# Attention scores in two 64-row halves, and scores, values and turns at the head of each slot

## The reference

```python
x = x + fast_weights(layernorm(x))      # 16 steps in order: z, y = x@t_k.T, x@t_v.T; one gradient step
                                        # on W1, b1, W2, b2 from mean((z + gelu(z@W1.T+b1)@W2.T+b2 - y)**2);
                                        # then the updated network on x@t_q.T
x = x + block(layernorm(x))

def block(x):                           # 16 heads, 4 key/value heads, 64 features a head
    q, k, v = split(rmsnorm(x) @ qkv_w + qkv_b)
    q, k = rope(q), rope(k)
    logits = q @ k.T / sqrt(64)         # a key at most 128 tokens back, none ahead
    attn = exp(logits - logaddexp(logsumexp(logits), attn_sink))
    x = x + (attn @ v) @ proj_w + proj_b
    h2 = rmsnorm(x)                     # then 4 of 32 experts for each token
    gw, e = softmax(top4(h2 @ gate_w + gate_b))
    return x + sum(gw * (silu(g) * u) @ W_down[e])    # u, g = halves of h2 @ W_up[e]
```

## Time and profile before

| | |
|---|---|
| time of the kernel, median of 3 runs | 1179.05 us (1175.15 to 1180.01) |
| profiled execution: span from first to last instruction | 1177.7 us (no other time of this execution is recorded) |
| PE busy, PEld busy | 981.5 us (83%), 716.8 us (61%) |
| DVE busy | 844.2 us (72%) |
| ACT busy | 629.5 us (53%) |
| POOL busy | 484.6 us (41%) |
| mean granted TensorE clock | 0.929 of full speed |

### The profile page before, as it was taken

How to read it: one execution, slowest core, us unless ns; L and a number is a source line. 1 busy time by engine, 2 the same in 40 slices (tenths; PEclk the granted TensorE clock), 3 DMA queues, 4 the chain that set the end, 5 groups by cost and what they waited for, 6 DMA issues and landing times. The chain is left out here.

```text
span 1177.7 us, 21481 instructions
## 1 busy us (share of the span) xinstructions
PE 981.5 (83%) x6262; PEld 716.8 (61%) x6356; DVE 844.2 (72%) x3032; ACT 629.5 (53%) x2211; POOL 484.6 (41%) x644
## 2 busy tenths in 40 slices
PE   4789999999999999899999989998895598797700
PEld 2446767666666666676666767666463487686600
DVE  3548898989888898989889898987883344333307
ACT  1027665665757576665757666575662155444300
POOL 2221214342433424243342534334234277777760
PEclk7799999999999999999999999999997699889955
DMA  5910000000000000000000000000083244443129
GB/s 143 265 29 1 2 1 21 1 21 1 21 11 11 19 3 21 1 21 8 14 15 7 21 1 20 7 15 19 3 300 131 71 129 131 133 113 99 54 67 334
DMA packets 65541, 67.29 MB, mean 57 GB/s; under 512 B 14961, under 2 KB 50706, under 8 KB 65426
## 3 DMA queue, kind: packets, MB, share of 16 engines
q1 hardware_dynamic: 51858, 44.13, 12.6%
q0 software_dynamic: 9216, 19.68, 4.9%
q10 hardware_dynamic: 4352, 2.10, 0.6%
HBM read 30.34 MB, written 35.52 MB: 56 GB/s over the span
## 5 line engine op out<-in xcount | busy, mean ns | idle before, releaser
L1137 POOL TENSOR_TENSOR l_t_cos<-l_t_cos,l_t_sin 128x512 f32<-128x512 f32 (+1 forms) x96 | 104.1, 1085 | 390.7 <-DVE l_t_sin L830 390.7
L1002 ACT ACTIVATE l_prob<-l_score,l_nm 128x256 f32<-128x256 f32 (+1 forms) x512 | 213.1, 439 | 1.8 <-DVE l_nm L697 1.5
L1331 POOL DMA_INDIRECT expert_out<-e_yo,e_dest x160 | 153.2, 957 | 68.8 <-issue 37.2
L1013 ACT COPY l_probT<-l_turned 128x512 f32<-128x512 f32 x192 | 112.9, 588 | 126.3 <-PE l_turned L388 125.7
L690 DVE TENSOR_REDUCE l_mx<-l_score 128x2 f32<-128x512 f32 (+1 forms) x192 | 131.6, 685 | 53.3 <-PE l_score L372 46.4
L96 POOL DMA_INDIRECT expert_rows<-h,slot x128 | 126.6, 989 | 47.7 <-issue 34.6
L388 PE MATMUL l_turned<-ident_sb,l_prob 128*128 128x128 f32 x768 | 122.8, 283 | 25.1 <-DVE l_prob L679 25.1
L679 DVE TENSOR_SCALAR l_prob<-l_prob,l_rec 128x256 f32<-128x256 f32 (+1 forms) x512 | 136.8, 321 | 6.8
L372 PE MATMUL l_score<-l_kpad,l_qT 128*128 128x512 f32 x256 | 131.5, 595 | 3.0
L404 PE MATMUL l_turned<-l_probT,l_vv 128*64 128x128 f32 x1536 | 126.5, 286 | 2.3 <-ACT l_probT L1013 2.3
L404 PEld LDWEIGHTS l_turned<-l_probT,l_vv 128*64 128x64 f32 x1536 | 80.0, 136 | 66.8 <-ACT l_probT L1013 39.7
(11 more groups left out here) (243 smaller groups left out, 1969.4 us busy)
## 6 DMA issues: line engine op xcount, KB each, us to landing
expert_rows<-zeros SPq DMA_DIRECT2D x32, 350.0 KB
e_xt<-expert_rows SPq DMA_DIRECT2D x160, 70.0 KB
e_rows<-expert_out SPq DMA_DIRECT2D x16, 512.0 KB, 5.9
wup_sb<-in_wup SPq DMA_DIRECT2D x1, 4096.0 KB, 14.7
expert_out<-e_yo,e_dest POOLq DMA_INDIRECT x160
expert_rows<-zeros SPq DMA_DIRECT2D x32, 70.0 KB, 2.4
expert_rows<-h,slot POOLq DMA_INDIRECT x128, 2.3
out_x<-e_res ACTq DMA_DIRECT2D x16, 128.0 KB, 6.1
```

What stands on the lines that cost most here:

```text
L1002: ins = A_.activation(prob[:, b, cols], score[u % 3][:, cols], ACT.Exp, bias=nm[:, b, j:j + 1], scale=0.125, accum_out=sums[:, b, j:j + 1])
L1013: A_.copy(probT[:, u % 2, :], turned[u % 2][:]).then_inc(s["probT"], 1)
L1137: g.tensor_tensor(t_cos[:, c % 2, 0:w], t_cos[:, c % 2, 0:w], t_sin[:, c % 2, 0:w], ALU.add).then_inc(s["added"], 1)
L1331: g_.indirect_dma_start(m["ys"], bass.IndirectOffsetOnAxis(ap=dest[:, g % FOUND, j:j + 1], axis=0), yo[:, g % YO, j, :], None).then_inc(se ...
```

## The change

Scores become two matmuls of 64 rows. `mask(u)` starts the tile; `half_scores(u, 0)` multiplies partitions 0 to 63 of the queries with head A's keys into the left half of the tile, `half_scores(u, 1)` partitions 64 to 127 with head B's into the right half. Neither reads the zeros of `kpad`. In slot u the program issues the mask and head A's half of unit u + 3, and beside it head B's half of unit u + 2, which goes to another bank. Head B's half signals that a tile is done. In tiles of the first queries the four blocks now stand head by head, so `nm`, `es` and the block numbers in `values` follow.

On PE the order inside a slot becomes scores, values, turns, and then `qkv`, the side stages and `qk_turn`. On ACT it becomes `exps(u + 1)`, `take_y(u - 1)`, `take_probs(u)`. DVE's order stays.

```diff
--- before.py
+++ after.py
@@ -292,7 +292,7 @@
             "stat small norms hn hn_ps hT qkv_ps cos sin added qk_ps qk_out v_out "
-            "s_ps mx nm es_in exped den rec normed t_ps probT y_ps yT "
+            "half_ps s_ps mx nm es_in exped den rec normed t_ps probT y_ps yT "
             "proj_ps xx x2 ss rms2 h2 h2_ps h2T gate_ps glog top w_in wexp wrec idx idxf hot picked rank_ps "
             "place prod masksum slotf slot x_sum counted").split()
@@ -355,28 +355,39 @@
             def bias(dst, c0, c1):
                 mm(dst, m["ones_bf"][:], m["bias3"][:, c0:c1], start=True, stop=False)
-            def scores(n, par, u):
+            def mask(n, par, u):
                 A, ap, u, done = at_unit(n, par, u)
                 if not live(A):
                     return
-                pairs, second, _ = unit(u)
-                g2 = pairs[0] // 4
-                dst = score[u % 3]
                 if u == 0:
                     pe.wait_ge(s["qk_out"], A * CHUNKS + 4)
                 if u == 6 or (u == 2 and A == 0):
                     pe.wait_ge(s["qk_out"], A * CHUNKS + CHUNKS)
                 after(pe, s["exped"], done - 3)
+                mm(score[u % 3][:], m["ident_bf"][:], (m["mask2"] if unit(u)[1] else m["mask1"])[:],
+                   start=True, stop=False)
+            def half_scores(n, par, u, hh):
+                A, ap, u, done = at_unit(n, par, u)
+                if not live(A):
+                    return
+                pairs, second, _ = unit(u)
+                g2, rows = pairs[0] // 4, slice(hh * DH, (hh + 1) * DH)
+                dst = score[u % 3][:, hh * 2 * P:(hh + 1) * 2 * P]
+                if hh == 1:
+                    pe.wait_ge(s["half_ps"], done)
                 if second:
-                    mm(dst[:], m["ident_bf"][:], m["mask2"][:], start=True, stop=False)
-                    mm(dst[:], qT[:, ap, pairs[0], P:TOK], kpad[:, ap, g2, :, :], start=False, stop=True) \
-                        .then_inc(s["s_ps"], 1)
+                    ins = mm(dst, qT[rows, ap, pairs[0], P:TOK], kpad[rows, ap, g2, hh, :], start=False, stop=(hh == 1))
                 else:
-                    mm(dst[:], m["ident_bf"][:], m["mask1"][:], start=True, stop=False)
                     for k, p in enumerate(pairs):
-                        ins = mm(dst[:, k * 2 * P:(k + 1) * 2 * P], qT[:, ap, p, 0:P], kpad[:, ap, g2, :, 0:P],
-                                 start=False, stop=(k == 1))
-                    ins.then_inc(s["s_ps"], 1)
+                        ins = mm(dst[:, k * P:(k + 1) * P], qT[rows, ap, p, 0:P], kpad[rows, ap, g2, hh, 0:P],
+                                 start=False, stop=(hh == 1 and k == 1))
+                ins.then_inc(s["s_ps"] if hh else s["half_ps"], 1)
+            def scores(n, par, u):
+                mask(n, par, u + 3)
+                half_scores(n, par, u + 3, 0)
+                half_scores(n, par, u + 2, 1)
             def turn_probs(n, par, u):
                 A, ap, u, done = at_unit(n, par, u)
@@ -398,7 +409,7 @@
                 for k in range(2):
                     for hh in range(2):
                         g = 2 * g2 + hh
-                        blk = 2 * hh + k if second else 2 * k + hh
+                        blk = 2 * hh + k
                         dst = turned[u % 2][hh * DH:(hh + 1) * DH, 0:P] if second else \
                             turned[u % 2][hh * DH:(hh + 1) * DH, k * P:(k + 1) * P]
                         ins = mm(dst, vv[:, ap, k if second else 0, g * DH:(g + 1) * DH],
@@ -632,22 +643,23 @@
             def iteration(n, par):
                 for u in range(UNITS):
-                    scores(n, par, u + 2)
+                    last_first = n == 2 and u == UNITS - 1
+                    if not last_first:
+                        scores(n, par, u)
+                    values(n, par, u - 1)
+                    turn_probs(n, par, u)
                     if n == 2 and u == 0:
                         qkv(n, par, 0)
                     if n == 2 and u % 2 == 0 and u < UNITS - 2:
                         qkv(n, par, u // 2 + 1)
                     elif n != 2 and u % 2 == 0:
                         qkv(n, par, u // 2)
-                    if u > 5 and u % 2 == 1:
-                        values(n, par, u - 1)
                     for stage in side.get(u, []):
                         stage(n, par)
-                    if not (u > 5 and u % 2 == 1):
-                        values(n, par, u - 1)
                     if u % 2 == 1:
                         qk_turn(n, par, u // 2)
-                    turn_probs(n, par, u)
+                    if last_first:
+                        scores(n, par, u)
                     if n < 3 or n == SEQS + 3:
                         keep_clock(1, turned[0] if n < 3 else score[2])
@@ -685,7 +697,10 @@
                 if live(A):
                     cols = unit(u)[2]
                     b, w = u % 2, cols.stop - cols.start
-                    sink = m["negsink"][:, cols]
+                    sink = m["negsink"][:, cols].rearrange("p (k h) -> p h k", h=2)
+                    def heads(tile):
+                        return tile[:, b, 0:w].rearrange("p (h k) -> p h k", h=2)
                     v.wait_ge(s["s_ps"], done)
                     V.tensor_reduce(mx[:, b, 0:w], score[u % 3][:].rearrange("p (h k) -> p h k", h=w), AX.X,
                                     ALU.max).then_inc(s["mx"], 1)
@@ -694,10 +709,10 @@
                 if live(A):
                     v.wait_ge(s["mx"], done)
-                    V.scalar_tensor_tensor(out=nm[:, b, 0:w], in0=mx[:, b, 0:w], scalar=-0.125, in1=sink,
+                    V.scalar_tensor_tensor(out=heads(nm), in0=heads(mx), scalar=-0.125, in1=sink,
                                            op0=ALU.mult, op1=ALU.min).then_inc(s["nm"], 1)
                     v.wait_ge(s["nm"], done)
-                    V.tensor_tensor(es[:, b, 0:w], nm[:, b, 0:w], sink, ALU.subtract).then_inc(s["es_in"], 1)
+                    V.tensor_tensor(heads(es), heads(nm), sink, ALU.subtract).then_inc(s["es_in"], 1)
             def x_norm(n, par):
@@ -1112,9 +1127,9 @@
             def iteration(n, par):
                 for u in range(UNITS):
-                    take_probs(n, par, u - 1)
-                    take_y(n, par, u - 2)
                     exps(n, par, u + 1)
+                    take_y(n, par, u - 1)
+                    take_probs(n, par, u)
                     if u in (0, 2):
                         v_out(n, par, u // 2)
                     if u % 2 == 1:
```

## The result

The changed kernel takes 1352.07 us (median of 4 runs, 1347.82 to 1353.77) against 1178.43 us of the kernel before beside it: a ratio of 1.1471, 95% interval 1.1451 to 1.149. The profiled span is 1350.6 us, 172.9 longer than before.

The account below looks back on a forecast made before the run. DVE was taken to bound the kernel: 47.25 us active plus 11.5 of waits gave 58.75, clock falls of 3.2 made 61.95, 10.0 more an iteration. 120 + 20 - 2 = 138 on 1179 gave 1317 us, range 1245 to 1360.

Parts of the forecast that it names:

- The rope loop: Even slots: DVE's rope waits for `qkv`, now behind the turns; 1.98 less 0.60 covered, 1.38 each, 8.3 an iteration.
- PE late in slots 2 and 4: PE reaches the turns late, 1.8 in slot 2 and 0.3 in slot 4, together 2.1 us an iteration.
- The gate's 0.7: Slot 7: `pick` waits for the gate, which now stands behind the turns; 0.7 us an iteration.
- The old waits: DVE's earlier waits for POOL and ACT, kept at 0.4 an iteration; those for scores were to go.
- DVE's active time: DVE's iteration time outside waits, 51.95 - 4.7 = 47.25 us, taken to stay the same.
- the prediction's own signs of being wrong: DVE's waits under 4.7 an iteration, `qkv` starting before `normed`, or DVE's active time leaving 47 us.
- The clock, 3.2: Falls after PE's pauses: 1.4 in slot 6, 0.6 each at slots 7, 9, 11; one fall at most 1.7.
- Three shorter iterations: Iterations 3, 16 and 17, with the same six rope waits but fewer side stages: 20 us at two thirds.
- the first rival: Rope waits without the clock's falls: 12 x 6.8 + 14 - 2 = 94 more, 1273 us; chance 0.22.
- The halves: PE's two 64-row score matmuls run side by side, 1.50 a unit for 1.79: 0.29 saved, mostly where PE waits anyway.
- The rival that the lighter PE wins: Slots 1 to 4, where DVE waits for PE: 3.5 us an iteration saved, 1134 us; chance 0.06.
- ACT's order at nothing: ACT's new order only makes its copies earlier, with ACT busy 33.45 of 51.95: priced at nothing.

Follow-up runs that it names:

- the filled kernel: The changed kernel with 10, 5, 8 and 7 extra matmuls ahead of PE's wait for the turns of slots 5, 7, 9 and 11: 1272.9 us, ratio 1.0811.
- the last kernel above: The kernel before, full-width scores, with DVE's rope ahead of the maxima in slots 0, 6, 8 and 10: 1167.95 us, ratio 0.9919.

## Why the prediction was right

It named the right mechanism and the right side, and 1352 lies in its range above the forecast of 1317. By its steps:

- **The rope loop, 1.38 an even slot: right.** Where PE is in time (slots 0, 6, 8 and 10 at full clock) the wait is 1.29; the 1.98 from the maxima to the rope were 1.97, and of these the maxima cover 0.68, not the 0.60 that the prediction took off. The six are 8.0 for the predicted 8.3, PE's lateness in slots 2 and 4 included. Moving `qkv` alone gives most of the time back.
- **PE late in slots 2 and 4, 2.1: right in place, a little high.** Slot 2 has 1.4 as a wait of the maxima for scores and a rope wait of 1.51, 0.2 above 1.29; slot 4 has 1.38, 0.1 above. Together 1.8. So the sentence that waits on scores would be gone was wrong: 8.0 us of two iterations are such waits, the rest of them behind falls of the clock. The gate's 0.7 is 0.63.
- **The old waits, 0.4: too high** (none is left in the list). All waits at full clock are 10.1, not 11.5.
- **DVE's active time, 47.25: too low** by 0.6 at full clock (57.97 less 10.1) and by 0.9 in the changed kernel (63.15 less 15.0 is 48.1). This is one of the prediction's own signs of being wrong, and it came. Its cause stays open. `es` is longer in the mean (598 ns, before 513; 16 us over 192 of them), as it now meets all six additions of POOL in an iteration. But before, the sixth fell on L795, the scaling of `l_hn`, which is shorter now (L810: 335 ns, before 773; 14 us over 32), so the two nearly cancel.
- **The clock, 3.2: the term that was mis-sized; it is 5.2.** The step that failed took 1.7 for the most that a fall can cost. Against the filled kernel, slot by slot, DVE's waits in the two iterations grow by 2.4 (slot 0), 1.5 and 2.5 (slot 6), 1.3 (7), 1.0 (8) and 1.0 (10). The longer falls at slots 5 and 11 cost more than 1.7: 3.8, in slots 6 and 7 of the longer iteration together, and 2.4 in slot 0. At slots 7 and 9 the price of 0.6 held in the mean: 1.0 each, in every other iteration.
- **Three shorter iterations, 20: measured 33.8** (12.2, 13.1, 8.5). Against the filled kernel the falls hold 17.9 of it; the 15.9 left are near the 14 that the first rival had for them. Iteration 18 gave 0.3 in place of -2, and 4.3 lie at the attention's start and in the experts, which the sum did not have. With 14.5 from the twelve full iterations, 13.8, 2.3 and 4.3 make the 34.9 by which the forecast was short. In the full iterations part of the closeness is luck: waits 1.4 too high stand against a clock 2.0 and an active time 0.6 too low.
- **The halves: right.** Side by side, 1.53 a unit for 1.50. Their 0.29 helps where PE has no reserve, three places an iteration by the prediction: 0.87, measured 0.73 at full clock. The rival that the lighter PE wins failed worse than its chance said, since under the new order, at the granted clock, the lighter PE loses.
- **ACT's order at nothing:** in the changed kernel no matmul of the two iterations waits for ACT, so the price holds there, but not for the reason given. It holds because PE's order changed with it.

The rival without falls of the clock, 1273, is what the filled kernel measured (1272.9); this is luck, as its twelve full iterations were together 9 us too dear and the rest as much too cheap.

The Trainium skill (TensorE: Matmul & The Clock Gate, Part 3), which the prediction named for a rival, says that matmuls on distinct row groups run at the same time. The trace after agrees with its starts of 427.27 and 427.28.

## What to carry to other kernels

Before a stage is moved behind an instruction that waits, look for who waits for that stage: if it is the engine that releases the wait, a loop closes, and its price is the sum of the stages in it less what still covers them. When two engines wait for each other in turn, price PE's pauses too, as the lower clock behind them cost here two thirds of what the rope loop did, and work saved on PE can make them longer. Orders of two engines that hand work to each other are one edit: ACT's half alone cost 31 us here, and PE's without it cost 61 more than both.

## What the runs showed of the hardware

The small DVE instructions with two inputs in SBUF that meet POOL's two-input addition here stand until it is done. In the changed kernel's slot 4:

```profile
428.60 1.26 POOL L1152 TENSOR_TENSOR l_t_cos<-l_t_cos,l_t_sin 128x512 f32<-128x512 f32 x1 [3.77 <-DVE l_t_sin L845]
428.61 1.26 DVE L715 TENSOR_TENSOR l_es<-l_nm,negsink 128x2 f32<-128x2 f32 x1
```

Two columns take 1.26 us, to the end of POOL's own 1.26, and 0.16 where POOL rests; the maxima, which read PSUM, keep 0.68 beside such an addition in the last kernel above. With the rope behind `nm` and `es` the drag does not go but moves on: `es` falls to 162 ns in the mean, and the square sums (L868) rise from 289 to 653 and L905 from 288 to 760. It is not only two tensors that are caught: L795 before, with one tensor and two numbers for each row, took 1.27 us beside the addition (442.12) and 0.33 without. The Trainium skill (SBUF — State Buffer, "SBUF: two separate sides") calls the port pair that the two engines share an exclusive lock: of a POOL operation that reads SBUF and a DVE operation with two SBUF inputs, the one that starts first holds it for its whole instruction. The trace agrees: POOL starts at 428.60, DVE at 428.61, and both take 1.26.

Not expected either: 30 filling matmuls an iteration made a kernel 79 us faster, and under the new order the scores in halves, whose matmuls have half the columns, were 27 us slower than the full-width ones.
